# Filling the upper copy of head 0's score stack straight from SBUF

## The reference

```
q = heads(xn @ wq.T + bq); k = heads(xn @ wk.T + bk); v = heads(xn @ wv.T + bv)
q2 = sum(q * q, -1); k2 = sum(k * k, -1)
d2 = maximum(q2[..., :, None] + k2[..., None, :] - 2 * einsum('bhid,bhjd->bhij', q, k), 1e-12)
attn = softmax(-sqrt(d2)); out = einsum('bhij,bhjd->bhid', attn, v); out @ wo.T + bo
```

## Time and profile before

| | |
|---|---|
| median of 3 runs | 1486.84 us (1486.05 to 1487.32) |
| profiled execution, its time | 1486.19 us |
| its span, first to last instruction | 1484.5 us |
| ACT busy | 1450.1 us (98%) |
| DVE busy | 1245.5 us (84%) |
| PE busy | 1121.4 us (76%) |
| first score clamp on DVE | 33.20 us |
| last clamp of round 0 ends | 69.49 us |

### The profile page before, as it was taken

One profiled execution on the slowest core, in us unless ns is written; L12 is line 12 of the kernel. 1 busy time (PEld: TensorE's weight loads), 2 busy tenths in 40 slices (PEclk: granted clock), 3 DMA queues, 4 the chain that ended last, 5 costly groups with the idle time before them and its releaser, 6 DMA issues.

```text
span 1484.5 us, 21370 instructions
## 1 busy us (share of the span) xinstructions
PE 1121.4 (76%) x7881; PEld 441.7 (30%) x7910; DVE 1245.5 (84%) x2236; ACT 1450.1 (98%) x792; POOL 413.7 (28%) x305
## 2 busy tenths in 40 slices
PE   5587786887887978878878774777677677776666
PEld 2123223243252442433424411232123222222212
DVE  7997978988989889789797787858898898988786
ACT  4899999999999999999999999999999999999998
POOL 5184460655503302123022130032123024022200
PEclk8598988999999999999999987899999999999999
DMA  4842644223242112121121420134033133021020
GB/s 130 240 131 61 177 127 124 52 57 84 79 135 69 51 43 53 43 56 52 43 66 30 95 74 18 32 107 87 27 112 84 27 112 83 27 91 48 21 70 20
DMA packets 104059, 112.71 MB, mean 76 GB/s; under 512 B 41722, under 2 KB 76026, under 8 KB 103946
## 3 DMA queue, kind: packets, MB, share of 16 engines
q1 hardware_dynamic: 98618, 99.47, 24.7%
q0 software_dynamic: 4464, 11.09, 2.7%
q10 hardware_dynamic: 864, 0.69, 0.2%
HBM read 66.52 MB, written 44.70 MB: 75 GB/s over the span
## 4 chain that ended last, share of the span: by engine, by line
ACT 69%; DVE 17%; issue 7%; PE 7%; DMA 1%; SPq 0%; DVEq 0%; ACTq 0%
ACT scores L719 25%; ACT scores L708 23%; ACT exp L1236 13%; DVE exp L1244 7%; DVE scores L683 6%; ACT exp L1232 3%; PE pvb L664 2%; ACT ht L969 1%; PE ring L649 1%; ACT L719 1%; ACT L708 1%; PE ring L426 1%; PE ring L930 1%; PE ring L1211 0%; DMA limit_full<-in_limit_full 0%
## 5 line engine op out<-in xcount | busy, mean ns | idle before, releaser
L683 DVE TENSOR_SCALAR scores<-ring 128x1024 f32<-128x1024 f32 x512 | 589.6, 1215 | 31.5 <-PE ring L649 31.3
L719 ACT ACTIVATE scores<-scores 128x8192 f32<-128x8192 f32 x64 | 445.8, 7021 | 0.2
L1236 ACT ACTIVATE exp<-ring 128x1024 f32<-128x1024 f32 x438 | 431.4, 1398 | 0.2
L708 ACT ACTIVATE scores<-scores 128x8192 f32<-128x8192 f32 x60 | 417.1, 7020 | 0.7 <-DVE scores L683 0.6
L1211 PE MATMUL ring<-stk 128*128 128x512 bf16 x995 | 299.5, 384 | 128.3 <-ACT exp L1236 106.6
L664 PE MATMUL pvb<-scores,val 128*9 128x256 f32 x4096 | 325.2, 392 | 89.9 <-ACT scores L719 44.0
L1244 DVE SCALAR_TENSOR_TENSOR exp<-exp 128x512 f32<-128x512 f32 x438 | 321.8, 757 | 62.1 <-ACT exp L1236 57.8
L649 PE MATMUL ring<-stk 64*128 64x512 bf16 x1024 | 210.3, 408 | 54.6 <-DVE scores L683 43.5
L1211 PEld LDWEIGHTS ring<-stk 128*128 128x128 bf16 x1024 | 65.7, 97 | 338.1 <-ACT exp L1236 241.8
L649 PEld LDWEIGHTS ring<-stk 64*128 64x128 bf16 x1024 | 49.8, 93 | 287.3 <-DVE scores L683 199.1
L664 PEld LDWEIGHTS pvb<-scores,val 128*9 128x9 f32 x4096 | 65.5, 89 | 219.4 <-issue 215.4
(11 more groups left out here) (252 smaller groups left out, 1178.8 us busy)
## 6 DMA issues: line engine op xcount, KB each, us to landing
stk<-stack SPq DMA_DIRECT2D x192, 192.0 KB, 2.9
stack<-qp SPq DMA_DIRECT2D x7, 768.0 KB, 4.4
stack<-kp SPq DMA_DIRECT2D x7, 768.0 KB, 5.7
xj<-xg SPq DMA_DIRECT2D x10, 448.0 KB, 4.2
yg<-yj POOLq DMA_DIRECT2D x10, 448.0 KB, 3.6
stack<-qp SPq DMA_DIRECT2D x7, 512.0 KB, 5.1
stack<-kp SPq DMA_DIRECT2D x7, 512.0 KB, 5.1
stk<-sum_rows SPq DMA_DIRECT2D x128, 24.0 KB
```

Source lines behind the costliest of these rows:

```text
L683: nc.vector.tensor_scalar(S[place][:, j * N:(j + 1) * N], tile, 1e-12, None, ALU.max).then_inc(o.release(("qk", group, place, j)), 1)
L708: nc.scalar.activation(S[place][:], S[place][:], ACT.Sqrt).then_inc(root_done, 1)
L719: nc.scalar.activation(S[place][:], S[place][:], ACT.Exp, scale=-1.0).then_inc(exp_done, 1)
L1236: nc.scalar.activation(EX[k // 2][:, k % 2, :], tile, ACT.Exp, scale=SCALE1).then_inc(o.release(("qk1", n, i)), 1)
```

## The change

A second way to fill partitions 0 to 53 of `stk0[0]` for head 0 only: every row is copied from `qp0`, `kp0`, `sump` and `ones_rows` in SBUF, as soon as its part is ready. There are 12 row copies (8 channels x 2 KB each), 6 copies of a sum row and 2 of three rows of one, 20 in all (`DIRECT`), all counted by one semaphore. 17 are issued by SP, ahead of or among its stores; 3, the sum rows of the Q side, by ACT at the end of `act_first`. The stores to DRAM stay as they are. `load_first_stack(0)` loads the lower copy alone. The first `ALONE` = 6 tiles of head 0 wait for the 20 copies and take both halves from the upper copy; tiles 6 and 7 take both copies as before and wait for the lower one.

```
 def store_rows(side, parts, part, ready, count):
     sp.wait_ge(ready, count)
+    direct_rows(sp, side, parts, part)
     store_part(sp, dst[0:n], side, parts, part, first_rows, 0, n)
...
+sp.wait_ge(zeroed, 1)
+direct_ones(sp)
 store_rows(Q, qp0, 0, q_heads, 2)
...
 sp.wait_ge(sum_half, 1)
+for part in range(2):
+    direct_sums(sp, K, part)
 store_first_sums(slice(0, 2))
 sp.wait_ge(sump_ready, 1)
+direct_sums(sp, K, 2)
 store_first_sums(slice(2, 3))
...
 # end of act_first
+act.wait_ge(zeroed, 1)
+act.wait_ge(sum_heads, 2)
+direct_sums(act, Q, 0)
+act.wait_ge(sum_half, 1)
+direct_sums(act, Q, 1)
+act.wait_ge(sump_ready, 1)
+direct_sums(act, Q, 2)
...
+DIRECT, ALONE = 2 * (len(PAIRS) + 3 + 1), 6
+def direct_rows(sp, side, parts, part):
+    rows = PART_ROWS[side][part]
+    for pair in range(rows.start, rows.stop, rows.step or 1):
+        sp.dma_start(stk0[0][pair:SUM_ROW:len(PAIRS), side, :], parts[0:HD, part, :]).then_inc(direct_in, 16)
+def direct_sums(eng, side, part):
+    row = SUM_ROW + 3 * side + part
+    eng.dma_start(stk0[0][row:row + 1, side, :], sump[32 * side:32 * side + 1, part, :]).then_inc(direct_in, 16)
+def direct_ones(sp):
+    for side in (Q, K):
+        row = SUM_ROW + 3 * (1 - side)
+        sp.dma_start(stk0[0][row:row + 3, side, :], ones_rows[0:3, 0:N]).then_inc(direct_in, 16)
 def load_first_stack(eng, n):
     eng.wait_ge(zeroed, 2)
     eng.wait_ge(first_rows, 96)
-    for side in SIDES:
+    sides = SIDES if n else SIDES[1:]
+    for side in sides:
         load_parts0(eng, n, side, n, stk_in[n])
     eng.wait_ge(first_sums, 64)
-    for side in SIDES:
+    for side in sides:
         load_sums0(eng, n, side, n, stk_in[n])
...
 def pe_scores0(pe, o, group, place, j):
-    slot = place % 2
-    if j == 0:
-        pe.wait_ge(stk_in[slot], 64 * (2 * group + place // 2 + 1))
+    slot, alone = place % 2, group == place == 0 and j < ALONE
+    if alone and j == 0:
+        pe.wait_ge(direct_in, 16 * DIRECT)
+    elif j == (0 if group or place else ALONE):
+        pe.wait_ge(stk_in[slot], 64 * (2 * group + place // 2 + 1) - (0 if slot else 32))
     tile = o.begin(pe, ("qk", group, place, j))
-    for side, cols in zip(SIDES, HALVES):
+    for side, cols in zip(SIDES[:1] * 2 if alone else SIDES, HALVES):
```

More of the change, by code:

```diff
@@ L297, in build @@
         first_rows, first_sums, ang_steps = (sem(n) for n in ("first_rows", "first_sums", "ang_steps"))
+        direct_in = sem("direct_in")
         q_stored, k_stored, sum_stored, v_stored = (
```

## The result

The changed kernel takes 1491.12 us (median of 9 runs, 1490.24 to 1492.48), the one before, run beside it, 1487.28 (9 runs). The ratio is 1.0026, with a 95% interval of 1.0018 to 1.0034: slower by 3.8 us, where 2.0 us less was forecast. The profiled execution took 1490.68 us, its span is 1489.0 against 1484.5.

What follows compares the result with a forecast made beforehand. ACT was taken to bound the kernel, its end set by VectorE's first clamp: 30.08 + 0.05 + 1.04 + 0.03 = 31.20 us against 33.20. So 1486.84 - 2.00 = 1484.84 us, range 1483.4 to 1487.6.

Steps and rivals of the forecast that it cites:

- The bound and the lever: Round 0: ACT runs without pause from about 69.5 us, so the end moves with VectorE's first clamp, at 33.20.
- The issue pitch: SP's queue: each added issue was taken at 0.363 us, from row stores back to back; last copy issued at 28.36.
- The added issues up to there cost nothing: SP's queue before 24.22 us: the added copies fit into idle time, with K part 0 ending at 22.46.
- the slower rival: SP's queue: issues cost more each, so 18 follow on one another from 21.01; slower from 0.52 us each; chance 0.1.
- its two prices: SP's cost per issue in that rival: 0.6 us, giving 1488.6 us in all, or 0.68 us, giving 1489.7.
- The flight: From the last copy's issue to its landing in the stack: 1.72 us, taken from an 8 KB store; landed at 30.08.
- The serial pair: TensorE, first six tiles: two matmuls in turn from one half take 1.04 us, 0.42 more than side by side.
- the clock: TensorE at the first tiles: granted clock 0.50 (1.2 GHz), taken to be the same a little earlier.
- TensorE's readiness: TensorE is past its branch on the flag between 28.5 and 30.2 us, just not late for the copies.
- Head 1's stack: Ahead of tile 8: SP's branch takes 3.69 us, the load lands by 39.35, needed by 39.57, so 0.22 us in hand.

Runs made afterwards that it cites:

- experiment 5: The changed kernel run again with nothing altered, for a second profile: 1491.82 us (one run).
- experiment 6: The changed kernel with two (in a further kernel four) small loads more in SP's idle time: 1489.44 us, ratio 1.0013 (four: 1489.87 us, 1.0014).
- experiment 7: The changed kernel with each store to DRAM ahead of the copies and K's sum copies behind all sum stores: 1489.62 us, ratio 1.0015.
- experiment 9: The changed kernel with stores first and its copies shared out over SP, ACT and POOL: 1486.19 us, ratio 0.9993 to the kernel before.
- experiment 10: As experiment 9, with part 2 of both sums issued by POOL instead of ACT: 1485.60 us, ratio 0.9990 to the kernel before.
- experiment 4: The kernel before, without copies, head 0's first six tiles taking both halves from the upper copy: 1487.30 us, ratio 1.0003.
- the two tests of shapes: The kernel before with test transfers of various shapes and ends in SP's idle time: 1486.25 us and 1487.64 us (one run each).
- experiment 8: The changed kernel without row copies, upper rows loaded from DRAM first, ACT issuing all six sum copies: 1486.29 us, ratio 0.9991 to the kernel before.

## Why the prediction was wrong

- **The bound and the lever: right.** The end hangs on the first clamp and on the unbroken row of clamps behind it. Taking first clamp plus the delay at head 1 for every kernel profiled, from 32.59 to 39.86 us, the span stands 1450.8 to 1452.2 us behind it.
- **The issue pitch: the step that failed.** "I take 0.363" came from stores to DRAM, one behind another, and stood for transfers that have both ends in SBUF. A row copy takes 0.62 to 0.64, its neighbour 0.44 to 0.70, and one copy of a sum row 1.41. "The added issues up to there cost nothing" fell with it: K part 0 wasn't through at 22.46 but at 23.40, after which nothing was idle. The last copy went out at 32.85 and not 28.36, 4.49 us late. That was the slower rival's mechanism, 18 issues from 21.01, with p = (32.85 - 20.93) / 18 = 0.66: inside its two prices, but it had 0.1 of the chance, since the rows against it were all of the wrong kind. They had DRAM at one end.
- **The flight: mis-sized.** 1.72 was taken; from 32.85 to TensorE's start it was 2.68, less the 0.05 of hand-over 2.63, 0.91 more. Experiments 5, 6 and 7 show 1.8 to 2.1 for the same copy, 9 and 10 3.27 from ACT and 4.23 from POOL with three engines at work. 4.49 + 0.91 = 5.40, less the 2.00 forecast as gain: 3.40, the measured delay.
- **The serial pair, the clock and TensorE's readiness: right.** 1.04 us (experiment 4), granted clock 0.50 in that stretch, and TensorE waited for the copy, not for its branch.
- **Head 1's stack: the place right, the price not.** "So 0.22 us in hand" was too thin. The sum load was out 5.0 us later than forecast (36.17 for 31.13), which the first clamp's own delay, 5.4 us (36.60 for 31.20), covers; what made head 1 late is the branch, taken over at 3.69 from the kernel before and 5.60 here, 1.91 more. Experiment 6 takes the 1.9 away, and VectorE no longer waits. In the change it cost 1.05 us.
- **The shape of the rivals.** The slower rival had the mechanism and the price of an issue. What it came to, 1488.6 and 1489.7, already lay above the range, which ends at 1487.6; so the 3.40 us alone put the result outside. It fell short of 1491.12 because it kept the flight at 1.72 and counted 0.3 us for head 1's stack at its lower price and nothing at its higher one, where 1.05 was lost.

On the Trainium skill: "DMA: Bandwidth & Descriptors", section "Issuing engines are not separate DMA queues", says that issuing from several engines saves only the sequencer's time, "which is usually small relative to the DMA itself". Here that time was most of the matter: 11.9 us of SP's issues against 2.6 us of flight, and sharing them out brought the first clamp from 36.60 to 32.59. In experiments 9 and 10 the last flights were 3.3 and 4.2 us; whether that comes of transfers running on common engines or of the engine that issued them, no run separates.

Open: why the second of two single-row copies takes 1.4 to 1.7 us in some kernels and 0.67 with stores ahead; what the branch waits for. The medians of experiments 9 and 10 are 1.25 and 1.95 us under the kernel before (1.0 and 1.5 by the ratios), their first clamps only 0.6 earlier; with intervals of 1.3 us to either side the runs can't tell whether that is more than scatter.

## What to carry to other kernels

A way round DRAM isn't short if it is made of many small transfers: count what each issue takes on the queue it stands in, from a row with the same two ends, and add up every issue from the last moment at which the queue was idle. If such a row doesn't exist, its absence should widen the forecast on the slow side, most of all where the queue is close to full and also carries the work that comes next. And when copies are worth having, put the stores that others wait for first and share the copies over the queues that are idle then; here that turned 3.4 us lost at the first clamp into 0.6 won.

## What the runs showed of the hardware

- In the two tests of shapes SP's issue of a transfer within SBUF took 0.55 to 0.81 us, whether it had 1, 8, 16 or 32 rows; with DRAM at one end 0.28 or 0.29, but 0.54 and 0.56 right behind one within SBUF. Single issues took much longer: the second copy of a sum row 1.41 us in the change, and the two copies of three rows of one, right behind the 384 KB stores at 5.46 us, 1.73 and 1.90. With two small loads ahead of them (experiment 6) those took 0.68 and 0.88.
- POOL issued the same 8-row copies in 0.50 to 0.58 us; their landing took 2.3 us or more, and that of its last single row 4.2.
- A pair of matmuls of 512 columns took 0.61 to 0.63 us from both halves of the rows side by side and 1.04 in turn from one half, both at a granted clock of 0.50.
- The same branch on SP took 3.6 to 3.7 us in nine of the thirteen profiles, 4.1 in one (experiment 8) and 5.6 to 6.2 in three (the change twice, and the stores first, which has as many instructions ahead of it). With two instructions more ahead of it, it took 3.65 us.
- A load of 48 rows of 4 KB from DRAM, the first in its queue and with another right behind it, took 3.87 us to land, hardly less than the two halves and the sums together (from 28.02 to 32.50, 4.48 us).
